# Second block of a two-block transformer kernel: the key-bias term of each query from VectorE, a row product with the normalised tile, in place of TensorE's row and fifth score product

## The reference, cut to what matters

```python
h = film(rmsnorm(x, norm1_w), cond, film1_w, film1_b)    # scale and shift for each sequence
Q = h @ q_w + q_b
K = h @ k_w + k_b
V = h @ v_w + v_b
scores = jnp.einsum('bnd,bmd->bnm', Q, K) * D ** (-0.5)
attn = jax.nn.softmax(scores, axis=-1)
out = jnp.einsum('bnm,bmd->bnd', attn, V)
x = x_in + (out @ proj_w + proj_b)
```

## Time and profile before

| | us |
|---|---|
| median of 3 runs | 1545.44 (1542.65 to 1545.99) |
| profiled execution | 1544.12 |
| its span, first to last instruction | 1542.2 |
| TensorE busy | 1517.2 (98%) |
| VectorE busy | 785.4 (51%) |
| ScalarE busy | 593.3 (38%) |
| GpSimd busy | 581.1 (38%) |

### The profile page before, as it was taken

One profiled execution on the slowest core, in us unless ns is written; L12 is line 12 of the kernel. 1 busy time (PEld: TensorE's weight loads), 2 busy tenths in 40 slices (PEclk: granted clock), 3 DMA queues, 4 the chain that ended last, 5 costly groups with the idle time before them and its releaser, 6 DMA issues.

```text
span 1542.2 us, 24532 instructions
## 1 busy us (share of the span) xinstructions
PE 1517.2 (98%) x8992; PEld 1234.6 (80%) x8992; DVE 785.4 (51%) x1616; ACT 593.3 (38%) x1884; POOL 581.1 (38%) x504
## 2 busy tenths in 40 slices
PE   5999999999999999999999999999999999999999
PEld 3888888888887667888878888888888888888887
DVE  5677777777766674555555443242424233252522
ACT  4656565656554455555554322121212121121210
POOL 5657666676654544534453302021211102121100
PEclk9999999999999999999999999999999999999999
DMA  7122222222126234333433210020102002020100
GB/s 258 56 84 82 83 90 78 95 77 90 62 77 232 69 142 146 104 96 104 136 123 126 73 62 22 1 78 3 69 13 68 14 0 82 0 75 7 54 1 28
DMA packets 60237, 117.87 MB, mean 76 GB/s; under 512 B 6352, under 2 KB 10448, under 8 KB 60144
## 3 DMA queue, kind: packets, MB, share of 16 engines
q1 hardware_dynamic: 60144, 116.65, 22.5%
HBM read 91.33 MB, written 25.30 MB: 76 GB/s over the span
## 4 chain that ended last, share of the span: by engine, by line
PE 96%; POOL 2%; DMA 1%; DVE 1%; issue 0%; SPq 0%; POOLq 0%
PE bank L587 27%; PE bank L589 26%; PE bank L588 26%; PE bank L666 4%; PE bank L659 2%; PE bank L677 2%; PE bank L962 2%; PE bank L718 1%; PE bank L883 1%; PE bank L709 1%; PE bank L611 1%; PE bank L986 1%; POOL xa L1747 1%; DMA xa<-xt_in 1%; PE bank L905 0%; PE bank L965 0%
## 5 line engine op out<-in xcount | busy, mean ns | idle before, releaser
L1706 DVE CAST g_hi<-gf 128x512 fp32r<-128x512 f32 x128 | 68.3, 533 | 427.4 <-ACT gf L1270 427.4
L1270 ACT ACTIVATE gf<-bank,cols 128x512 f32<-128x512 f32 x128 | 88.3, 690 | 512.7 <-PE bank L589 512.7
L1105 ACT ACTIVATE pa<-bank,neg_max 128x128 f32<-128x128 f32 x512 | 181.7, 408 | 135.0 <-DVE neg_max L1377 135.0
L587 PE MATMUL bank<-w_hi,g_hi 128*128 128x512 f32 x512 | 200.5, 392 | 0.0
L587 PE MATMUL bank<-hb_hi,w_hi 128*128 128x512 f32 x512 | 199.3, 389 | 0.3 <-DVE vb_lo L1293 0.3
L589 PE MATMUL bank<-w_hi,g_lo 128*128 128x512 f32 x512 | 199.4, 389 | 0.0
L588 PE MATMUL bank<-w_lo,g_hi 128*128 128x512 f32 x512 | 199.2, 389 | 0.0
L589 PE MATMUL bank<-hb_hi,w_lo 128*128 128x512 f32 x512 | 199.2, 389 | 0.0
L588 PE MATMUL bank<-hb_lo,w_hi 128*128 128x512 f32 x512 | 199.2, 389 | 0.0
L1756 POOL TENSOR_TENSOR xrc<-xrc,b 128x512 f32<-128x512 f32 x32 | 48.1, 1532 | 304.7 <-DMA xrc<-x_dram 304.7
L1782 POOL TENSOR_TENSOR pa<-pa,rec 128x512 f32<-128x512 f32 x128 | 132.3, 1042 | 54.4 <-DVE rec L1400 54.3
(11 more groups left out here) (201 smaller groups left out, 3155.8 us busy)
## 6 DMA issues: line engine op xcount, KB each, us to landing
rows<-st_dram SPq DMA_DIRECT2D x32, 512.0 KB, 4.3
xb<-x_dram SPq DMA_DIRECT2D x60, 256.0 KB, 3.0
xa<-xt_in SPq DMA_DIRECT2D x32, 256.0 KB, 4.3
xra<-xt_in SPq DMA_DIRECT2D x32, 256.0 KB, 2.7
x_dram<-h SPq DMA_DIRECT2D x32, 256.0 KB, 2.0
xrb<-x_dram SPq DMA_DIRECT2D x32, 256.0 KB, 3.4
stage_w<-w_in SPq DMA_DIRECT2D x16, 512.0 KB, 3.8
x_dram<-xrb SPq DMA_DIRECT2D x32, 256.0 KB, 2.3
```

Source lines behind the costliest of these rows:

```text
L587: nc.tensor.matmul(dst, w_hi, a_hi, start=start, stop=False)
L1105: last = nc.scalar.activation(pa[:, j, m, :], scores_bank[j][:, m * P:(m + 1) * P], ACT.Exp, bias=neg_max[:, j * C + m:j * C + m + 1], acc ...
L1270: nc.scalar.activation(gf[f % 2][:], bank[f % 2][:], ACT.Gelu, bias=cols[:, B1_COL + f:B1_COL + f + 1])\
L1706: nc.vector.tensor_copy(g_hi[:, r, :], gf[f % 2][:]).then_inc(g_hi_ready, 1)
```

## The change: what it does

The first group keeps the old way. For groups 1 to 7 the query term h·u + const is rewritten: h is the normalised tile xn times a scale plus a shift, so h·u is the product of row xn with the vector u times scale of that sequence, plus a constant of the sequence. The 32 vectors (`u_tab`) and the constants (`cst`) are made once, at the start of stage B: VectorE makes the tables, TensorE transposes them (`u_transpose`, after the first `h_g` of group 0), ScalarE copies the rows, and SyncE writes them to DRAM (`u_dram`). For each sequence of groups 1 to 7 SyncE reads one row back, spread over all 128 partitions (`load_u_row`, 256 KB written, two buffers), and VectorE multiplies it with xnb and sums along the row (`query_bias`). The sum goes into the bias of the exponential (two small instructions for a group, and one more for each sequence). `h_u`, the copy rb and the fifth product are left out in groups 1 to 7.

```diff
+            def load_u_row(t):
+
+                wait(sp, rq_made, t - GB - 1)
+                sp.dma_start(u_row[:, t % 2], u_dram[t:t + 1, :].partition_broadcast(P))\
+                    .then_inc(rows_ld[t % 2], 16)
...
                 load_bxr(g, GB - 1)
+                if not last:
+                    load_u_row(GB * (g + 1))
+                    load_u_row(GB * (g + 1) + 1)
                 if first:
                     load_w1(0)
...
                     load_w1(g + 1)
+                if not last:
+                    load_u_row(GB * (g + 1) + 2)
+                    load_u_row(GB * (g + 1) + 3)
                 store_x2(g, 0)
...
+            def u_transpose():
+
+                pe.wait_ge(cst_made, 1)
+                for c in range(C):
+                    nc.tensor.transpose(bank[3][0:NB, c * P:(c + 1) * P], u_tab[:, c, :], ident[:])
+                nc.tensor.matmul(bank[2][:, 0:NB], inv_hd[:].broadcast_to([P, P]), u_sum[:, 1, :], start=True,
+                                 stop=True).then_inc(uc_t, 1)
...
-                    if m == 2:
+                    if m == 0 and first:
+                        u_transpose()
+                    if m == 2 and first:
                         h_u(g)
...
+                    if first:
+                        last = nc.tensor.matmul(ps_s[b % 2][:, 0:P], rb[:, tok], inv_hd[:].broadcast_to([P, P]),
+                                                start=False, stop=True)
+                    last.then_inc(bs_done, 1)
...
+            def query_bias(t):
+
+                dve.wait_ge(bxn, t + 1)
+                dve.wait_ge(rows_ld[t % 2], 16 * (NB // 2 + (t - GB) // 2 + 1))
+                wait(dve, rq_made, t - GB)
+                nc.vector.scalar_tensor_tensor(u_junk[:], xnb[:, t % GB], 1.0, u_row[:, t % 2], ALU.mult, ALU.mult,
+                                               accum_out=rq[:, t // GB % 2, t % GB:t % GB + 1]).then_inc(rq_made, 1)
...
+            def whole_query_bias(g):
+
+                dve.wait_ge(rq_made, GB * g)
+                i = g % 2
+                then(nc.vector.tensor_tensor(rq_full[:, i, 0, :], rq[:, i, :], cst[:, GB * g:GB * (g + 1)], ALU.add))
+                then(nc.vector.tensor_scalar(rq_full[:, i, 1, :], rq_full[:, i, 0, :], INV_SQRT_D, None, ALU.mult))
...
+                    if not first and not last and m >= 2:
+                        query_bias(GB * (g + 1) + m - 2)
...
+                if not first:
+                    whole_query_bias(g)
...
+                    else:
+                        r_sum, r_scaled = (rq_full[:, g % 2, i, b:b + 1] for i in range(2))
+                        then(nc.vector.tensor_scalar(bias, raw, r_sum, INV_SQRT_D, ALU.subtract, ALU.mult))
+                        nc.vector.tensor_tensor(bias, bias, r_scaled, ALU.add).then_inc(bmax, 1)
...
+                    if first or (b < 2 and not last):
+                        query_bias(GB * (g + 1) + (b if first else b + 2))
```

More of the change, by code:

```diff
@@ L221, in block_pair_kernel @@
         stage_w1 = run("stage_w1", [P, 2, C, FF // NG])
+        u_row = run("u_row", [P, 2, D])
+        u_tab = run("u_tab", [P, C, NB])
+        u_part = run("u_part", [P, NB, C])
+        u_rows = run("u_rows", [NB, D])
+        u_sum = run("u_sum", [P, 2, NB])
+        cst = run("cst", [P, NB])
+        rq = run("rq", [P, 2, GB])
+        rq_full = run("rq_full", [P, 2, 2, GB])
+        assert run.offset <= stage_w1_at + 16 * kib
         run.offset = stage_w1_at + 16 * kib
@@ L228, in block_pair_kernel @@
         uc_rows = fv1
+        u_junk = at("u_junk", [P, D], BF16, st_at)
         run = Run(R0)
@@ L301, in block_pair_kernel @@
         var2_ready, ln2_shifted, x1_ready = sem("var2_ready"), sem("ln2_shifted"), sem("x1_ready")
-        raw_in = [sem(f"raw_in{i}") for i in range(4)]
+        raw_in = [sem("raw_vp_in"), sem("raw_qk_in")]
+        rq_made, cst_made = sem("rq_made"), sem("cst_made")
         film_in = [sem("film_in1"), sem("film_in2")]
@@ L961, in body_b @@
                     for k in range(C):
[L962 to L966, removed]
+                        last = nc.tensor.matmul(ps_s[b % 2][:, 0:P], tb[:, k, tok], hb[:, k, tok], start=(k == 0),
+                                                stop=(k == C - 1 and not first))
+                    if first:
+                        last = nc.tensor.matmul(ps_s[b % 2][:, 0:P], rb[:, tok], inv_hd[:].broadcast_to([P, P]),
+                                                start=False, stop=True)
+                    last.then_inc(bs_done, 1)
                     if b < GB - 1:
@@ L1630, in body_b @@
                         end_a(m)
+                    if first and m == 0:
+                        dve.wait_ge(uc_t, 2)
+                        nc.vector.tensor_scalar(cst[:], bank[2][:, 0:NB], float(HD), None, ALU.mult).then_inc(cst_made, 1)
+                    if not first and not last and m >= 2:
+                        query_bias(GB * (g + 1) + m - 2)
                     if m < 2:
@@ L1643, in body_b @@
                     dve.wait_ge(braw, t + 1)
-                    nc.vector.tensor_scalar(neg_max[:, 2 * (b % 2) + 1:2 * (b % 2) + 2], neg_max[:, 2 * (b % 2):2 * (b % 2) + 1], INV_SQRT_D, None, ALU.mult)\
-                        .then_inc(bmax, 1)
+                    raw, bias = (neg_max[:, 2 * (b % 2) + i:2 * (b % 2) + i + 1] for i in range(2))
+                    if first:
+                        nc.vector.tensor_scalar(bias, raw, INV_SQRT_D, None, ALU.mult).then_inc(bmax, 1)
+                    else:
+                        r_sum, r_scaled = (rq_full[:, g % 2, i, b:b + 1] for i in range(2))
+                        then(nc.vector.tensor_scalar(bias, raw, r_sum, INV_SQRT_D, ALU.subtract, ALU.mult))
+                        nc.vector.tensor_tensor(bias, bias, r_scaled, ALU.add).then_inc(bmax, 1)
                     if b == 0:
```

35 lines of the change are left out of this document (25 added, 10 removed).

## The result

| | before | after |
|---|---|---|
| median us | 1545.44 (1542.06 to 1545.99, 5 runs) | 1598.37 (1596.71 to 1599.91, 5 runs) |
| span of the profiled execution | 1542.2 | 1598.0 |
| mean granted clock of TensorE | 0.997 | 0.986 |

The ratio is 1.035, with the interval 1.0335 to 1.0365: the kernel became 3.5% slower, 53 us by the medians and 55.8 by the two spans. The forecast was +40 and a range up to 1599, so the median lies inside the range by 0.6 us.

A forecast was written before the change was run, and what follows sets the result against it. TensorE, busy for 98%, was taken as the bound. On 1544.12: +1.6 `u_transpose`, +4.5 group 0 to 1, +33.8 five periods, +1.3 group 6 to 7, -0.9 group 7, together +40: 1584.4 profiled, 1585 median; range 1563 to 1599.

The forecast's parts named there:

- the period of groups 1 to 6: Stage B, first scores of one group to the next: 39.3 us against 32.55, five periods +33.8.
- the first lap: Stage B, after a group's first scores (S): exponential 1 at S + 9.7 us, residual of tile 1 at S + 20.05.
- the row's landing: Groups 1 to 6, from SyncE's issue of the row load to its arrival: 3.3 us, ends 2.5 and 4.3.
- The new wait: VectorE waits for SyncE's row, quarter 3 of tb behind it; TensorE idle about 5.0 us in each of six groups.
- `u_transpose`: Transposes and a product of 32 columns added to TensorE once, in group 0: +1.6 us.
- The clock: After each longer wait in stage B TensorE's clock is at 0.50, with 1.6 us lost.
- Group 7: Last group of stage B: no row to wait for, its fifth products left out, -0.9 us.
- The saving: TensorE without `h_u` (1.21 us) and four fifth products (0.22 each): 2.1 us a group, 14.7 for seven groups.
- Group 0's wait: TensorE's 3.7 us wait in group 0 moves along with the added transposes and stays.
- all dearer: Rival: row lands in 4.3, each sum costs 0.19, clock down 1 us longer; about +55, 1600 us; chance 0.18.

## Why the prediction was right in kind and short in size

The step that failed is the period of groups 1 to 6 in the sum, 39.3 and measured 41.35, so that five periods brought +44.0 and not +33.8. Two of its terms were too small: the first lap (from S to the residual of tile 1 I had 20.05, measured 21.4) and the row's landing (3.3, measured 4.1). The mechanism was the one forecast. That the range still held the median, by 0.6 us, is luck: it was drawn for the landing's two ends, and nothing in it stood for the first lap.

- **The new wait.** Right, and shown: where, how often, what hangs on it, and that SyncE's order sets it (the two kernels with the row earlier). Forecast 5.0 us of idle TensorE in a group, measured 5.9 in the mean.
- **The landing.** Mis-sized. I took 3.3 from issue to product. Measured over the groups it was 3.84 to 4.57, some 4.1, so 0.8 too little in each period. From the residual of tile 1 to the row's issue were 14.1 to 15.0, 14.4 in the mean, as I had it (14.43). Whether the surplus is the broadcast form or the residual tile and the weights beside it no run separates; in one stretch of that wait, 743 to 744, the DMA engines were busy for 0.92 of the time.
- **The first lap.** Mis-sized, and the larger part. I had exponential 1 at S + 9.7; it came at 11.1 in the mean. In group 3 the copy of the values started at S + 6.05, against 5.9; in groups 5 and 6 it came at 7.16 and 6.65. From this copy to exponential 1 I used 2.88, which I had read from the second lap, and added 0.95. In the first lap that stretch took 3.52 already in the kernel before (the first lap was 6.06 there, and not 4.6), for the rounding was held beside GpSimd's addition (1.34 in place of 0.69): 0.64 of the miss. With the row product behind it, the same additions held rounding and product for 0.17 + 0.49 more in group 3. Together 1.3 in that group. With the additions moved, the stretch was 3.73, a little under my 3.83. The laps 2 and 3 were 5.48 and 4.86, against 5.55 and 4.85.
- **The period.** 0.7 from the chain through SyncE and 1.35 from the laps make the 41.35 that was measured (mean of five) out of the 39.3 forecast. Five times 2.05 is 10.3 of the 15.5 us by which the span missed. Of the rest, 4.7 lie in group 7, 1.4 between groups 6 and 7 (the first `h_g` of group 7 started at 20.25 after the scores, against 18.9: the same lap) and 1.1 in stage A, less 1.9 in group 0 and `u_transpose`.
- **The clock.** Right: down to 0.50, and 1.5 us dear in a group by the run with the extra products, against 1.6.
- **Group 7.** Not foreseen: +3.8 where -0.9 was forecast. In this group TensorE waited 3.46 before `transpose_pb`, and the scores behind it ran at half the clock again (1.92 for eight products, which are 1.06 otherwise). Read backwards: the exponential was at 870.54; before it DVE's second instruction of `whole_query_bias` (L1638), 0.17 long elsewhere, was held for 1.0 beside POOL's additions, and the last one of the bias for 0.44; before these stood `low_v`, behind the copy of the values, behind the squares of tile 3, for which ScalarE had waited 4.12 us. No run tests this by itself; it is read from these rows, of PE, ACT, DVE and POOL. The run with the additions early bears it out in part: in its group 7 the two instructions took 0.18 and 0.24, ScalarE waited 1.86 before the squares, the first exponential came 3.6 after the scores and not 7.2, and the stretch to the end was 2.0 shorter. The held instruction of 128x4 reads SBUF with one input, so two inputs do not cover every instruction that was held; whether it ran in a two-port mode no trace shows.

```profile
871.05 0.48 PE L955 MATMUL bank<-ident,pb 128*128 128x128 f32 x1 [3.46 <-ACT pb L1277]
871.32 1.92 PE L1001 MATMUL bank<-hb,tb 128*128 128x128 f32 x8
```

```profile
864.68 0.63 ACT L1167 ACTIVATE junk<-xb 128x512 bf16<-128x512 f32 x1 [4.12 <-issue]
```

```profile
868.11 1.18 DVE L1638 TENSOR_SCALAR rq_full<-rq_full 128x4 f32<-128x4 f32 x1
```

```profile
868.01 2.48 POOL L1834 TENSOR_TENSOR xrb<-xrb,cb 128x512 f32<-128x512 f32 x2
```

- **`u_transpose`.** Too dear by 0.9: 567.08 - 566.50 = 0.58 from its first transpose to the product behind it (rows in the last section), and 0.08 on the first one behind it. The first scores of group 0 came 0.67 later by it.
- **The saving.** 2.1 us a group was too much for the period: with the term gone it fell by 1.45, and by some 1.75 less its waits. `h_u` had its price, but what the last fifth product gave was lost around the start of the next group.
- **Group 0's wait.** I kept it at 3.7 with its fall of the clock. It was 2.19, and the clock stayed up. Group 0 to 1 cost 3.5 and not 4.5; that this is why was not tested.
- Of the rivals, "all dearer" (above 1591, with a chance of 0.18) is where the time fell. Its landing of 4.3 was right in direction, its 0.19 for each sum was not: the rows have 0.08, inside a product that is otherwise shorter. The rule that it named, two instructions for one with an accumulator, the trace shows. It had nothing on GpSimd's additions, so its nearness (1600) is luck as well.

## What to carry to other kernels

Before work is moved to an engine with time to spare, look up when its input arrives: an instruction that waits for a DMA is placed right only if the DMA's place in its queue, plus the landing, comes before everything that stands behind the instruction. Read the length of a lap from the same lap of the loop, not from its neighbour, and look at what GpSimd does in that stretch. And ask first whether the work is needed: the term that was moved at a cost of 53 us cancels in the softmax, and to leave it out gained 12.

## What the runs showed of the hardware that was not expected

- DVE and POOL took turns: 0.69 became 1.51, 1.18 or, in the kernel with the products behind quarter 3, 1.61, and POOL's 2.51 for two additions became 2.99. Even an instruction on 128 x 1 waited, 0.67 where it takes 0.16 (both rows from that kernel):

```profile
706.38 1.61 DVE L1630 SCALAR_TENSOR_TENSOR u_junk<-xnb,u_row 128x512 bf16<-128x512 f32 x1
...
708.49 0.67 DVE L1722 TENSOR_TENSOR neg_max<-neg_max,rq_full 128x1 f32<-128x1 f32 x1
```

- Four transposes with 32 stationary columns and a product of 32 columns ran in the stream without a gap, where `h_u`, narrow products into four different quarters of a bank, cost 1.21:

```profile
566.50 0.60 PE L938 MATMUL bank<-ident,u_tab 128*32 128x128 f32 x4
566.94 0.31 PE L939 MATMUL bank<-u_sum,inv_hd 128*128 128x32 f32 x2
567.08 0.47 PE L614 MATMUL bank<-hb_hi,g_hi_b 128*128 128x512 f32 x1
```

- After a wait of 2.19 us, in group 0, the clock was still up (TensorE took 3.94 from the transposes to `transpose_pb`, where it took 5.49 after 3.72 in the kernel before).
